# Scores before the query projection: the order of two groups of matmuls on TensorE in a six-layer windowed-attention kernel

## The reference, cut to what matters

```python
for i in range(DEPTH):                                  # 6
    x = attn_layer(shift_tokens(x), Wqkv[i], q_scale[i], k_scale[i], Wo[i]) + x
    x = ffn_layer(shift_tokens(x), ln_g[i], ln_b[i], W1[i], b1[i], W2[i], b2[i]) + x
...
def attn_layer(x, Wqkv, qs, ksc, Wo):
    qkv = x @ Wqkv                                      # q, k, v: 16 heads of 64
    q = l2norm(q) * qs
    k = l2norm(k) * ksc
    # rotary tables with a scale, then
    sim = einsum(q, k of this window and the one before) * QK_SCALE, masked
    out = softmax(sim) @ v
    return out @ Wo
def ffn_layer(x, g, bln, W1, b1, W2, b2):
    hg = layernorm(x) @ W1 + b1
    a, gate = split(hg)
    return a * gelu(gate) @ W2 + b2
```

## Time and profile before

| | |
|---|---|
| median of 3 runs | 1732.43 us (1731.41 to 1736.98) |
| profiled execution, first to last instruction (span) | 1731.0 us |
| TensorE busy | 1639.0 us, 95% of the span |
| VectorE busy | 1446.3 us, 84% |
| ScalarE busy | 1425.6 us, 82% |
| GpSimd busy | 1311.9 us, 76% |
| chain that ended last | TensorE 61%, ScalarE 28%, issue 6%, VectorE 4% |
| mean granted TensorE clock | 0.986 of full |

### The profile page before, as it was taken

How to read it: one execution, slowest core, us unless ns; L and a number is a source line. 1 busy time by engine, 2 the same in 40 slices (tenths; PEclk the granted TensorE clock), 3 DMA queues, 4 the chain that set the end, 5 groups by cost and what they waited for, 6 DMA issues and landing times.

```text
span 1731.0 us, 68758 instructions
## 1 busy us (share of the span) xinstructions
PE 1639.0 (95%) x25970; PEld 1277.2 (74%) x25970; DVE 1446.3 (84%) x3011; ACT 1425.6 (82%) x2851; POOL 1311.9 (76%) x1305
## 2 busy tenths in 40 slices
PE   7779999999999999999999999999999999999995
PEld 5657777777777777777777777777777777777773
DVE  4499888888888888888888888888888888888884
ACT  3367888888888888888888888888888888888885
POOL 6088877877877787787778778787877877777765
PEclk9799999999999999999999999999999999999997
DMA  4111111111111111111111111111111101111000
GB/s 140 41 38 43 35 33 36 30 48 38 41 32 30 36 36 42 49 30 32 30 36 42 49 36 30 32 30 48 38 41 36 30 27 38 35 30 32 28 24 26
DMA packets 41426, 66.40 MB, mean 38 GB/s; under 512 B 7072, under 2 KB 16032, under 8 KB 41376
## 3 DMA queue, kind: packets, MB, share of 16 engines
q1 hardware_dynamic: 40224, 65.38, 12.7%
q10 hardware_dynamic: 1152, 0.34, 0.1%
HBM read 20.61 MB, written 1.05 MB: 13 GB/s over the span
## 4 chain that ended last, share of the span: by engine, by line
PE 61%; ACT 28%; issue 6%; DVE 4%; ACTq 1%; DMA 0%; POOL 0%; DVEq 0%; POOLq 0%
PE ps_qs L530 12%; PE ps_po L530 9%; PE ps_q L530 8%; PE ps_a L530 7%; PE ps_tk L530 7%; PE ps_f L530 6%; PE ps_po L650 5%; ACT p_bd L943 4%; PE ps_k L530 4%; PE ps_v L530 4%; ACT squares L949 4%; ACT L1053 3%; ACT L1050 3%; ACT q_t L943 3%; ACT prob L987 2%
## 5 line engine op out<-in xcount | busy, mean ns | idle before, releaser
L427 POOL TENSOR_TENSOR qk<-qk,rnorm 128x512 f32<-128x512 f32 x384 | 393.6, 1046 | 176.6 <-DVE rnorm L1284 176.1
L419 POOL TENSOR_TENSOR qk<-qk,qk_rot 128x512 f32<-128x512 f32 x384 | 483.8, 1282 | 0.0
L434 POOL TENSOR_TENSOR prob<-prob,row_inv 128x512 f32<-128x512 f32 x192 | 200.7, 1045 | 92.8 <-DVE row_inv L1301 92.8
L1289 DVE TENSOR_REDUCE row_max<-ps_qs 128x8 f32<-128x512 f32 x191 | 132.0, 691 | 164.8 <-PE ps_qs L530 164.8
L943 ACT COPY p_bd<-ps_po 64x512 f32<-64x512 f32 x378 | 219.1, 580 | 58.8 <-PE ps_po L650 56.4
L1264 DVE TENSOR_REDUCE ssq<-squares 128x8 f32<-128x512 f32 x384 | 261.4, 681 | 3.4 <-ACT squares L949 3.4
L530 PEld LDWEIGHTS ps_qs<-k_t,q_t 64*32 64x32 f32 x12224 | 179.2, 107 | 69.0 <-issue 68.9
L943 ACT COPY attn_t<-ps_po 128x512 f32<-128x512 f32 x191 | 112.5, 589 | 133.2 <-PE ps_po L530 133.1
L530 PE MATMUL ps_qs<-k_t,q_t 64*32 64x64 f32 x12224 | 210.1, 218 | 0.0
L530 PE MATMUL ps_po<-p_bd,v_back 128*64 128x64 f32 x3056 | 193.2, 225 | 0.0
L530 PEld LDWEIGHTS ps_po<-p_bd,v_back 128*64 128x64 f32 x3056 | 163.1, 137 | 35.8 <-issue 17.0
(11 more groups left out here) (237 smaller groups left out, 4082.7 us busy)
## 6 DMA issues: line engine op xcount, KB each, us to landing
v_back<-v_own SPq DMA_DIRECT2D x192, 192.0 KB, 2.4
w_raw<-in_wqkv SPq DMA_DIRECT2D x48, 192.0 KB, 2.4
v_back<-v_own SPq DMA_DIRECT2D x96, 64.0 KB, 2.1
wo_sb<-in_wo SPq DMA_DIRECT2D x12, 256.0 KB, 2.9
w_sb<-in_w SPq DMA_DIRECT2D x6, 341.0 KB, 3.1
w_sb<-in_w SPq DMA_DIRECT2D x6, 192.0 KB, 2.7
x_in<-in_x SPq DMA_DIRECT2D x4, 256.0 KB, 4.2
out<-s_out SPq DMA_DIRECT2D x8, 128.0 KB, 1.9
```

The costliest lines, as they stand in the source:

```text
L419: nc.gpsimd.tensor_tensor(qk[:, s, i, :], qk[:, s, i, :], qk_rot[:, s, i, :], ALU.add).then_inc(added, 1)
L427: nc.gpsimd.tensor_tensor(heads(qk[:, s, i, :]), heads(qk[:, s, i, :]), rnorm[:, s, 8 * i:8 * i + 8].unsqueeze(2).to_broadcast([P, 8, HEAD ...
L434: nc.gpsimd.tensor_tensor(heads(prob[:, s, :]), heads(prob[:, s, :]), row_inv[:, s, :].unsqueeze(2).to_broadcast([P, 8, HEAD]), ALU.mult). ...
L1289: V.tensor_reduce(row_max[:, s, :], heads(ps[:]), AX, ALU.max).then_inc(max_done, 1)
```

## The change

The two calls change places. The query projection of unit u follows the scores of unit u - 3, in each slot of body(n). The order on ScalarE, VectorE, GpSimd and SyncE is the same as before, and no semaphore or value that is waited for differs.

```diff
             def body(n):
                 for j in range(UNITS):
                     u = UNITS * n + j
-                    project(n, j, 0, ps_q, q_scaled, q_done)
                     if live(u - 3):
                         scores(u - 3, (j - 3) % UNITS, (j - 3) % 2)
+                    project(n, j, 0, ps_q, q_scaled, q_done)
                     if live(u - 4):
                         turn_p(u - 4, j % 2)
                     project(n, j, 1, ps_k, k_scaled, k_done)
```

## The result

The changed kernel takes 1774.58 us (median of 4 runs, 1772.03 to 1777.56), the kernel before on the same chip 1734.41 (1731.41 to 1736.98). The ratio is 1.0236, 95% interval 1.0214 to 1.0259: slower by 40 us. The forecast was 1782.8, slower, in a range of 1752 to 1810.

A forecast was written before the change was run, and what follows sets the result against it. The prediction saw a loop of ScalarE (12.8 us) and TensorE (20.8) as the bound. It added 1.08 and 0.10 per iteration, times 44 51.9, less 1.5, to 1731.0; plus 1.4 for the runs' median: 1782.8 us, range 1752 to 1810.

The forecast's parts named there:

- the wait for k_t: TensorE's wait before slot 1's down projection, forecast to grow from 0.9 to about 2.0 us; otherwise the prediction is wrong.
- x: Gap on TensorE from V to the scores' load in the new order; taken as 0.42 us, bounds 0.21 and 0.56.
- a further wait costs about 0.085: Gap behind the value matmuls: 0.21 us with one semaphore wait, 0.38 with three, so each extra wait was priced at 0.085.
- The first rival: TensorE's gaps are the price of another matmul shape, not of waits: x 0.21, 1741.5 us, chance 0.15.
- The seam: TensorE's stretch from value matmuls to the turning of p: forecast to change by x - 0.42 us per slot.
- V: Start of the last weight load of a slot's value matmuls on TensorE, the point from which the prediction counts.
- The late squares: ScalarE's squares of ps_q in slot 1 wait for the later projection: x + 0.66, or 1.08 us later.
- The wait for the mask: In slot 3 the earlier scores wait for the mask under them: 0 to 0.2 us, taken as 0.10.
- The likeliest case: x from 0.34 to 0.49 us with 0.10 for the mask: 1769 to 1795 us, chance 0.56.
- The scores' waits cost what they cost now: Rival: the gap before the scores stays as long, x 0.56 us, mask wait 0.2: 1812 us, chance 0.22.
- faster: Rival: TensorE's sequencer clears the scores' waits during the value matmuls, x 0.02 us: 1708 us, chance 0.03.
- No difference: Rival: x near 0.15 us, or the squares' lateness is made good before k_t; chance 0.04.

The follow-up runs named there:

- Delaying the squares alone: Kernel before with TensorE's order kept; in slot 1 ScalarE's squares of ps_q also wait for that slot's scores: 1807.35 us, ratio 1.043.
- filling ScalarE's hole alone: Changed kernel with ScalarE's slot 1 table load moved ahead of the squares of ps_q: 1746.54 us, ratio 1.0076 to the kernel before.
- slot 2 alone: Kernel before with the scores put before the query projection in slot 2 only: 1728.34 us, one run.
- slot 3 alone: Kernel before with the scores put before the query projection in slot 3 only: 1728.12 us, ratio 0.9966.
- slot 1 alone: Kernel before with the scores put before the query projection in slot 1 only: 1781.94 us, ratio 1.028.

## Why the prediction was right, and what was off

The mechanism held at each of its places: the squares of slot 1 now follow the projection, ScalarE's slack was none, the wait for k_t grew to 1.9 (2.0 forecast), the mask became a wait in slot 3, VectorE's gain was worth nothing. Delaying the squares alone and filling ScalarE's hole alone showed in both directions that the wait ahead of ScalarE's work in slot 1 is what costs. The sizes were off in four terms, three of them from one misread row, and a fifth, the falls of TensorE's clock, wasn't in the sum.

*x, the gap behind the values.* The step "a further wait costs about 0.085" failed. It compared slot 0 with the other slots and took their number of waits for the difference. x is 0.21, the lower bound. The first rival named this value: its rule from the Trainium skill, TensorEngine Tiling (Array Packing), Key Properties, that a change of tiling mode drains TensorE, fits these traces. With one wait or three the gap at such a change is 0.21, the seam has lost one of three changes, and the periods of the kernels with slot 2 alone and slot 3 alone are 0.15 shorter. No run separates a drain from another cost of the change of shape.

*The seam.* Forecast 0 at x = 0.42, and -0.21 at x = 0.21. Measured from V to V in the changed kernel: slot 2 to 3 is 7.02 instead of 7.19, slot 0 to 1 is 8.40 instead of 8.58, so -0.17 and -0.18.

*The late squares.* Forecast +1.08, measured V + 2.26 less V + 1.35, +0.91; with x = 0.21 the formula gives 0.87. That ScalarE's lateness in slot 0 adds nothing to it held.

*The wait for the mask.* Forecast 0.10. Measured: the seam into slot 3 is 0.16 longer in all, which includes its own saving of 0.17, so 0.33; the gap behind V alone shows 0.50 less 0.21, 0.29. The earlier the scores come, the longer they wait for a mask that comes at its own time.

*The sum.* 1.18 was forecast for a period and 0.74 came; 0.91 - 0.17 - 0.18 + 0.16 is 0.72. Over the 44 distances from the first to the last down projection 0.74 each is 32.6 us. The rest of what lies between them is a term that the sum didn't have: six of these distances are 35.9 us instead of 34.37, together 9.2 us. They are falls of TensorE's granted clock. The stretch behind the down projection at 244.04, busy time and granted clock:

```profile
core 0: us, PE busy (x) PEld busy (x) DVE busy (x) ACT busy (x) POOL busy (x), PEclk, DMA share, GB/s
...
237.00:241.00 4.00, 4.00 (x39) 3.37 (x28) 2.36 (x6) 3.60 (x7) 3.04 (x3) 1.00 0.20 55
241.00:245.00 4.00, 2.09 (x16) 1.33 (x16) 3.95 (x8) 3.94 (x9) 3.15 (x4) 1.00 0.00 0
245.00:249.00 4.00, 4.00 (x103) 3.56 (x99) 1.81 (x5) 1.18 (x3) 3.75 (x4) 0.57 0.02 4
249.00:253.00 4.00, 4.00 (x34) 3.50 (x27) 3.24 (x8) 2.91 (x7) 1.41 (x3) 1.00 0.24 66
```

TensorE is busy for 2.09 of the 4 us from 241, and then the granted clock is 0.57 on average over 4 us, between 1.0 (2.4 GHz) and 0.5 (1.2 GHz). The prediction had named this fall as a sign of being wrong and had put no price on it: by that sign it failed here, while by the other one, the wait for k_t, it held. Before the first down projection 1.5 us were lost instead of won, which is less than the starts of these traces differ by, and 1.5 more after the last. 32.6 + 9.2 + 3.0 is the 44.8 of the spans.

That the time lies so near the forecast is partly luck. The likeliest case, 1769 to 1795, was tied to x from 0.34 to 0.49, and x was 0.21. The periods came out 19.3 us below the forecast (51.9 less 32.6); the falls gave back 9.2 and the two ends 4.5, which leaves the span 5.6 below the 1781.4.

*The rivals.* "The scores' waits cost what they cost now" needed x at 0.50 or more and "faster" 0.14 or less; both fall with x at 0.21. "No difference" falls with the time. The first rival was right in x and would have said 1741.5. By its period of 33.9 it was not proved: 34.37 came. It had 0.24 a period, and the 0.5 that it lacks are the mask (0.33), three seams that saved 0.17 or 0.18 and not 0.21 (0.11), and the squares (0.04). It had no falls either.

## What to carry to other kernels

Before instructions of one engine change places, ask which of the two another engine stands in line for, and whether that engine has slack there: work on ScalarE that came 0.9 us later in every iteration cost 40 us here (slot 1 alone cost 49, with eight falls of the clock), while the same exchange in slot 3 alone, where it was absorbed, won 0.3%. Two gains that each hold alone may not add up, when the first delays what the second brings forward. And a cost taken from the difference of two rows needs a third row in which only the supposed cause differs; it was in the same trace.

## What the runs showed of the hardware that was not expected

The granted clock fell in some periods only, and more often with a longer hole on TensorE before the down projection (the wait for k_t, by its longest value). With 0.9 to 1.5 us none of the 43 periods shows a fall, in nine kernels. With 1.9 us it was 6 of 43 in the changed kernel and 8 of 43 with slot 1 alone; with 2.2 us, the squares delayed alone, it was 15 of 43. A fall costs 1.5 us. Why it came in these periods and not in their neighbours, no run shows.

Semaphore waits that are met cost TensorE nothing that these traces can tell: one or three in front of the projection leave 0.21 us behind V. The step from the last weight load of the values (128x64) to the first of the projection (128x128) or of the scores (64x32) takes those 0.21 us, where the value loads themselves stand 0.03 apart. Whether the change of shape is the whole reason was not tried alone.
